# Making the low half of every second query head on TensorE and ScalarE instead of VectorE, in a one-core cross-attention and expert block

## What is computed

```python
qh, kh, vh = heads(layernorm(x), Wq), heads(ctx, Wk), heads(ctx, Wv)
scores = einsum('bhqd,bhkd->bhqk', qh, kh) + mask
probs  = softmax(scores)
x = x + tanh(g_xattn) * (einsum('bhqk,bhkd->bhqd', probs, vh) joined) @ Wo.T
xf = layernorm(x)
w, idx = top_k(softmax(xf @ Wg + bg), 2); w = w / sum(w)
y = relu(xf @ W1[e] + b1[e]) @ W2[e] + b2[e]         # for the two picked experts e
x = x + tanh(g_ffn) * sum(w * y)
```

## Time and profile before

| | before |
|---|---|
| median of 3 runs | 1154.45 us (1152.84 to 1154.65) |
| profiled execution, its own time | 1155.27 us |
| its span | 1153.5 us |
| PE busy | 881.5 us, 76% |
| DVE busy | 939.9 us, 81% |
| ACT busy | 785.6 us, 68% |
| POOL busy | 710.6 us, 62% |
| mean granted clock of TensorE | 0.921 |

### The profile page before, as it was taken

How to read it: one execution, slowest core, us unless ns; L and a number is a source line. 1 busy time by engine, 2 the same in 40 slices (tenths; PEclk the granted TensorE clock), 3 DMA queues, 4 the chain that set the end, 5 groups by cost and what they waited for, 6 DMA issues and landing times.

```text
span 1153.5 us, 33826 instructions
## 1 busy us (share of the span) xinstructions
PE 881.5 (76%) x11840; PEld 674.7 (58%) x11840; DVE 939.9 (81%) x2160; ACT 785.6 (68%) x1627; POOL 710.6 (62%) x701
## 2 busy tenths in 40 slices
PE   6787888798788888877897887878898767555560
PEld 4465665566566766666675656666676556444440
DVE  3888898898989897978888989978798987646633
ACT  3877778777677878786887667766887564444540
POOL 3143455547365666564658787755758787778775
PEclk9998899999999999999999998999998897778975
DMA  8367756555467765453445455554445465477773
GB/s 173 75 172 196 206 146 171 153 159 157 130 172 197 207 179 158 107 131 96 116 116 147 121 161 131 128 129 103 109 122 160 119 172 154 145 202 211 209 205 103
DMA packets 250791, 174.53 MB, mean 151 GB/s; under 512 B 39168, under 2 KB 232192, under 8 KB 250624
## 3 DMA queue, kind: packets, MB, share of 16 engines
q1 hardware_dynamic: 242432, 155.57, 50.9%
q0 software_dynamic: 8192, 16.79, 4.9%
HBM read 75.42 MB, written 63.84 MB: 121 GB/s over the span
## 4 chain that ended last, share of the span: by engine, by line
DVE 24%; issue 13%; PE 13%; POOL 8%; ACT 8%; SPq 3%; DMA 2%; DVEq 0%; POOLq 0%; ACTq 0%
PE bank L90 4%; POOL arena L1033 4%; PE bank L92 3%; PE bank L91 3%; DVE qL L726 3%; POOL hidL L1072 2%; DVE vL L901 2%; DVE row_max L929 2%; DVE otL L955 2%; DVE arena L909 2%; DVE x_back L949 2%; POOL slots L1020 2%; DVE row_sum L917 1%; SPq L1153 1%; ACT qH L545 1%
## 5 line engine op out<-in xcount | busy, mean ns | idle before, releaser
L1078 POOL TENSOR_TENSOR ptL<-pt,ptH 128x512 f16<-128x512 f32 x128 | 148.8, 1162 | 250.9 <-ACT pt L651 250.6
L726 DVE TENSOR_TENSOR qL<-bank,qH 128x512 f16<-128x512 f32 x256 | 173.7, 681 | 51.7 <-ACT qH L545 49.5
L545 ACT ACTIVATE qH<-bank 128x512 f16<-128x512 f32 x256 | 152.9, 599 | 43.8 <-PE bank L92 42.6
L1084 POOL TENSOR_TENSOR prob<-prob,row_inv 128x512 f32<-128x512 f32 x128 | 134.9, 1054 | 52.4 <-DVE row_inv L935 52.3
L1020 POOL DMA_INDIRECT slots<-x2hat,slot x128 | 128.1, 1001 | 31.9 <-issue 29.9
L90 PE MATMUL bank<-ptH,vdH 128*128 128x64 f16 x1024 | 120.4, 202 | 33.6 <-DVE arena L909 23.6
L1033 POOL DMA_INDIRECT arena<-slots,slot x128 | 123.1, 962 | 36.1 <-issue 29.7
L90 PE MATMUL bank<-arena,hidH 128*128 128x128 f16 x396 | 83.6, 240 | 69.6 <-POOL hidL L1072 66.9
L90 PEld LDWEIGHTS bank<-ptH,vdH 128*128 128x128 f16 x1024 | 107.9, 118 | 41.2 <-DVE arena L909 27.6
L1072 POOL TENSOR_TENSOR hidL<-arena,hidH 128x512 f16<-128x512 f32 x99 | 115.7, 1169 | 12.2 <-ACT hidH L595 10.8
L91 PE MATMUL bank<-ptL,vdH 128*128 128x64 f16 x1024 | 120.4, 202 | 0.0
(11 more groups left out here) (158 smaller groups left out, 3399.5 us busy)
## 6 DMA issues: line engine op xcount, KB each, us to landing
arena<-expert_weights SPq DMA_DIRECT2D x99, 321.0 KB, 3.1
slots<-zeros SPq DMA_DIRECT2D x60, 512.0 KB, 3.4
vdH<-vH SPq DMA_DIRECT2D x256, 64.0 KB
vdL<-vL SPq DMA_DIRECT2D x256, 64.0 KB
arena<-slots SPq DMA_DIRECT2D x99, 128.0 KB
slots<-arena SPq DMA_DIRECT2D x99, 128.0 KB
x_raw<-in_x SPq DMA_DIRECT2D x16, 256.0 KB, 4.1
ctx_raw<-in_ctx SPq DMA_DIRECT2D x16, 256.0 KB, 4.6
```

Source lines behind the costliest of these rows:

```text
L545: act.activation(qH[:, g % 2, 2 * j + g2, :, h2, :], bk("Q", g, h)[:, :].rearrange("p (b q) -> p b q", b=GB), ACT.Copy).then_inc(s_q_high, 1)
L726: dve.tensor_tensor(qL[at], bk("Q", g, h)[:, :].rearrange("p (b q) -> p b q", b=GB), qH[at], ALU.subtract).then_inc(s_q_low[h % 2], 1)
L1078: pool.tensor_tensor(ptL[:, b % 2, :], pt[:, b % 2, :], ptH[:, b % 2, :], ALU.subtract).then_inc(s_pt_low, 1)
L1084: pool.tensor_tensor(p, p, row_inv[:, b % NPB, :].unsqueeze(2).to_broadcast([P, JG, S]), ALU.mult).then_inc(s_normal, 1)
```

## The change

For odd heads the low half is made in another way. TensorE multiplies the high half that ScalarE has just written to SBUF (qH, 16 bit) by minus the identity and adds that to the bank, in which the head still stands; what is left in the bank is the remainder, and ScalarE copies it as the low half. VectorE's subtraction of the odd heads goes; the even heads stay as they were.

```diff
+        minus_ident = sb("minus_ident", [P, P], F16)
...
+            def queries_rest(g, h):
+                pe.wait_ge(s_q_high, g * H + h + 1)
+                if g == 0 and h == 1:
+                    pe.wait_ge(s_minus, 2)
+                j, h2, g2 = h // 4, h % 4 // 2, h % 2
+                pe.matmul(bk("Q", g, h)[:, :].rearrange("p (b q) -> p b q", b=GB), minus_ident[:, :],
+                          qH[:, g % 2, 2 * j + g2, :, h2, :], start=False, stop=True,
+                          skip_group_check=True).then_inc(s_q_rest, 1)
...
                 if within(s - 2, B):
                     transpose_probs(s - 2)
+                if within(g + 1, GROUPS):
+                    queries_rest(g + 1, 2 * i + 1)
                 if unit_at(s - 1) is not None:
                     hidden(unit_at(s - 1))
...
+            def queries_rest_low(g, h):
+                act.wait_ge(s_q_rest, g * H // 2 + h // 2 + 1)
+                j, h2, g2 = h // 4, h % 4 // 2, h % 2
+                act.activation(qL[:, g % 2, 2 * j + g2, :, h2, :], bk("Q", g, h)[:, :].rearrange("p (b q) -> p b q", b=GB),
+                               ACT.Copy).then_inc(s_q_low[1], 1)
...
                     act.activation(pt[:, b % 2, :], bk("PT", b)[:, :], ACT.Copy).then_inc(s_pt_out, 1)
+                if within(g + 1, GROUPS):
+                    queries_rest_low(g + 1, 2 * i + 1)
                 if unit_at(s - 1) is not None:
                     hidden_relu(unit_at(s - 1))
...
-                                  ALU.subtract).then_inc(s_q_low[h % 2], 1)
+                                  ALU.subtract).then_inc(s_q_low[0], 1)
...
-                if within(g + 1, GROUPS):
-                    queries_low(g + 1, 2 * i + 1)
...
+            pool.memset(minus_ident[:, :], 0.0).then_inc(s_minus, 1)
+            pool.wait_ge(s_minus, 1)
+            pool.affine_select(out=minus_ident[:, :], in_=minus_ident[:, :], compare_op=ALU.not_equal, fill=-1.0, base=0,
+                               pattern=[[-1, P]], channel_multiplier=1).then_inc(s_minus, 1)
```

More of the change, by code:

```diff
@@ L232, in flamingo_block @@
         s_wpe, s_xT, s_ctxT, s_x2T = sem("weights_pe"), sem("xT"), sem("ctxT"), sem("x2T")
+        s_q_rest, s_minus = sem("q_rest"), sem("minus_ident")
         s_q, s_v, s_scores, s_pt, s_pv, s_wo = (sem(n) for n in ("q", "v", "scores", "pt", "pv", "wo"))
```

## The result

| | before | changed |
|---|---|---|
| median of 4 runs | 1153.68 us (1152.84 to 1154.65) | 1197.64 us (1196.93 to 1198.1) |
| span of the profiled execution | 1153.5 us | 1195.9 us |
| mean granted clock of TensorE | 0.921 | 0.918 |

The change made the kernel slower: ratio 1.038, 95% interval 1.0362 to 1.0398. The direction was the predicted one, the size was not: 1197.64 lies outside 1144 to 1192 and is what the rival "the stops feed on one another" had given (1198, chance 0.14).

What follows compares the result with a forecast made beforehand. No engine bounds everything; in steps 6 and 1 ScalarE waits for VectorE. Start 5.5, six groups without experts 9, nine with 0: +14.5 us on 1155.3, 1169.8; the median 0.8 lower, so 1169, range 1144 to 1192.

Steps and rivals of the forecast that it cites:

- the stops feed on one another: Rival: TensorE, stopped twice a group, resumes at half clock with its queue behind it; 43 us more, 1198; chance 0.14.
- The start: Steps -8 to -1, before the first group: each head pair waits for ScalarE's copy; +5.5 us, ends 3 and 8.4.
- The odd head's copy and the wait in step 6: Group without experts, batch element 6: copy ends at 229.62, the product follows, probabilities times values starts 5.4 us later.
- The walk, 1.2 us a group without experts: Operations followed one by one through a group without experts: it ends 1.2 us later than before.
- The clock. ... I take 0.3: Low TensorE clock after longer gaps in steps 6 and 1: 0 to 2 us a group without experts, 0.3 taken.
- A group with experts ... = 0: An existing TensorE wait hides most of the new one: -1.8 + 1.8 = 0 for nine groups, ends -1.5 and +2 each.
- steps 2 to 5 give back 1.8 us a group: Groups with experts: steps 2 to 5 give back about 0.35 each and step 1 the same, 1.8 us together.
- VectorE is the bound after all: Rival: subtractions in steps 1 to 5 of all 15 groups come back whole; 24 us faster, 1131; chance 0.20.
- The rule of the highest occupancy: Both query stages: optimize the busiest engine first, VectorE at 88 and 89%; by it the time would fall.

Runs made afterwards that it cites:

- the filler: Throwaway 512-column products before TensorE's wait, first six groups: changed kernel, steps 6 and 1, 1.0231 (1.0328 without); kernel before with step 6's wait alone, 1.0065 (1.0132 without).
- step 6's wait alone: Kernel before plus TensorE's wait for ScalarE's copy of the odd head in step 6 (batch element 6, counted 0 to 7) of each group: 1.0132.
- Waits in steps 1 and 6: Kernel before plus TensorE's wait for ScalarE's copy of the odd head in steps 1 and 6 of each group (30 waits), no product: 1.023.

## Why the prediction was wrong in size

- **The start**: +5.5 predicted, +5.2 measured. Right.
- **The odd head's copy and the wait in step 6**: the copy's end came out to 0.01 us, the stop at 4.52 us (4 to 5 predicted). Right.
- **The walk, 1.2 us a group without experts**: 0.7 a group is left when the clock is kept up. Near, as far as one execution shows it, and with the reservation made above.
- **"The clock. ... I take 0.3"**: this failed. The low clock cost 1.8 us in step 6 of the group shown, and up to 2.6 us a group for steps 6 and 1 together (15.3 / 6 by the filler in the changed kernel, with the reservation made there; 8.4 / 6 = 1.4 for step 6's wait alone), where the term had 0.3 and an upper end of 2. The reason given was that two gaps of 2 us were in the rows already. It missed what the low clock falls on: before, VectorE and ScalarE had other work in it (4.00 of 4 us), while behind the longer stop they wait for just those products. The walk itself priced them at full speed (nine products of step 7, "9 x 0.215"); they stood 0.43 apart. The Trainium skill (TensorE: Matmul & The Clock Gate, the section on oscillation in real kernels) describes this pattern, a wait in every tile with the tile behind it at the low clock; there the wait is for a DMA, here it is for ScalarE, and the row of 244 to 248 us with its granted 0.50 agrees.
- **"A group with experts ... = 0"**: this failed too; +15.2 us for nine, inside its own end of +2 a group. It rested on one stop in one step 6, 2.92 us for a bank that VectorE frees, which was to hide the new wait. The waits of TensorE in the whole stage (line waited for: us in total, times, longest) show what happened. First before (346 to 900 us), then changed (366 to 932):

```profile
PE bank L90 <- DVE arena L909: 46.0, 31, 3.3
```

```profile
PE bank L355 <- ACT qH L558: 60.8, 53, 5.2
PE bank L90 <- DVE arena L930: 8.5, 8, 2.4
```

  The new wait did take the place of the old one (46.0 to 8.5), as predicted, but it is 60.8, not 46, and comes as two stops a group, 2.6 to 5.2 us before L355 in step 6 and 1.5 to 3.1 in step 1. In the group of the earlier trace rows the stop grew only to 3.27 us, much as predicted, and seven of the nine groups had such a stop of 2.75 to 2.93 us before. But two had no such stop there and got 2.58 and 5.21, and one went from 2.75 to 4.86: in all, step 6 went from 20.0 to 32.6 us and step 1 from 8.9 (six groups) to 16.2 (nine). Waits in steps 1 and 6 are 8.3 us of the 15.2, those in other steps 2.4; by difference the rest, 4.5 us, is the copy and product less the freed subtraction. Each of these is within twice the scatter of one execution, so this split is rougher than the first six groups'. The prediction also had steps 2 to 5 give back 1.8 us a group; the subtraction with nothing in its place gave only 5.8 us in nine groups, 0.6 a group.
- **"VectorE is the bound after all"** (0.20): refuted. Taking the subtractions away gave 1.2%, and ScalarE's copies cost 1.3%. The rule of the highest occupancy (the Trainium skill, Perfetto Trace Analysis, Identifying the Most-Contended Engine) did not hold here: VectorE had 88 to 89% and relieving it by 76 us was worth 14.
- **"The stops feed on one another"** (0.14): its mechanism, half clock with the queue behind it, is the one that the filler confirms for the six groups, at 3.3 instead of 4 us a group; its nine groups at 1.5 measured 1.7, but there the half clock was not tested. That its 1198 meets the measured time to the microsecond is partly luck: its six groups were 4 us too long, the nine and the rest that much too short. It was given too small a chance, although the products 0.43 us apart were on the table.

**What stays open.** The kernel before takes 1155 us in some sets and 1172 in others. Of the 16 us, 12.4 lie in the nine groups with experts (553.7 against 566.1) and 2.9 in the rest. There, ScalarE shows a wait that the list of the 1155 us execution does not have:

```profile
ACT ptH L648 <- remote: 40.3, 16, 4.5
```

"remote" is the profile's word for a release that it can put down to no instruction. Such waits stand in all 14 traces that go with a kernel before of 1171 to 1172 us and in none of the other six; what lies behind them is not known. It touches both kernels, since all ratios are within a set. In which operations of the groups with experts the low clock acts was not separated from the plain lateness either; the filler ran in the first six groups only.

## What to carry to other kernels

Before a wait is put into the queue of an engine that runs ahead, add up what stands behind it: here the same work without the wait cost 0.5%, with it 3.3 to 3.8%. When the added wait makes TensorE stand for 3 to 5 us, as in steps 1 and 6 here, price the products behind it at 1.2 GHz as well, and look whether another engine waits for exactly those; if the stop can't be avoided, products that are thrown away during it took back most of the loss of these groups. A stop read in one group is no cover for all of them: sum old and new wait over the stage, step by step, first.

## What of the hardware was not expected

- Products whose results are thrown away made a kernel faster: 20 products of 512 columns (4.48 us) within a known stop brought the next 4 us from a granted 0.66 to 1.00 (the kernel before has a stretch of 0.63 there itself), and the kernel from 1.0132 to 1.0065 of the time of before.
- A mean granted clock tells little of this loss: 0.921 before and 0.918 changed over the span, with 0.50 exactly where it hurts. Two kernels with 0.93 over the first stage took 301.7 and 319.9 us for its six groups; VectorE was busy in 66% of the half clock of the slower one.
- The same kernel before took 1155.46 us in one set of runs and 1171.13 to 1172.48 in four others, each set on a chip of its own.
